# First attention: probabilities as TensorE's weights, values moving, no transposes of outputs, ten probability buffers

## The reference, cut to what matters

```python
qm, km, vm = (_split_heads(...) for ...)            # (4, 16, L, 8)
scores = jnp.einsum('bnlh,bnph->bnlp', qm, km) / np.sqrt(HEAD_DIM)
scores = jnp.where(mask, scores, MASK_FILL)
attn = jax.nn.softmax(scores, axis=-1)
out = jnp.einsum('bnlp,bnph->bnlh', attn, vm)
...
return out @ Wo.T + bo
```

## Time and profile before

| | before |
|---|---|
| median of 3 runs | 597.49 us (597.3 to 597.72) |
| profiled execution, its own time | 596.67 us |
| its span, first to last instruction | 594.9 us |
| mean granted clock of TensorE | 0.997 |
| TensorE busy | 569.7 us (96%) |
| VectorE busy | 401.7 us (68%) |
| ScalarE busy | 322.5 us (54%) |
| GpSimd busy | 105.4 us (18%) |

### The profile page before, as it was taken

One profiled execution on the slowest core, in us unless ns is written; L12 is line 12 of the kernel. 1 busy time (PEld: TensorE's weight loads), 2 busy tenths in 40 slices (PEclk: granted clock), 3 DMA queues, 4 the chain that ended last, 5 costly groups with the idle time before them and its releaser, 6 DMA issues.

```text
span 594.9 us, 8098 instructions
## 1 busy us (share of the span) xinstructions
PE 569.7 (96%) x2512; PEld 374.7 (63%) x2512; DVE 401.7 (68%) x1265; ACT 322.5 (54%) x566; POOL 105.4 (18%) x120
## 2 busy tenths in 40 slices
PE   4899999999999999999999899999899999999997
PEld 3556666665566667656676466666666676666664
DVE  6888989774132344666637585777889999768564
ACT  1587688766454476644855348745292542342321
POOL 3111110000111311242202432126201110100000
PEclk9999999999999999999999999999899999999999
DMA  4400000300311100101111011061321233341431
GB/s 119 195 15 10 18 10 2 105 39 19 107 36 35 54 20 19 36 28 54 60 31 44 14 42 44 1 199 39 122 75 51 90 119 98 111 138 62 143 120 56
DMA packets 23306, 38.35 MB, mean 64 GB/s; under 512 B 3776, under 2 KB 9536, under 8 KB 22880
## 3 DMA queue, kind: packets, MB, share of 16 engines
q1 hardware_dynamic: 22832, 37.44, 19.9%
q10 hardware_dynamic: 432, 0.40, 0.2%
HBM read 36.45 MB, written 1.38 MB: 64 GB/s over the span
## 4 chain that ended last, share of the span: by engine, by line
PE 80%; DVE 10%; ACT 4%; issue 2%; POOL 2%; DMA 1%; DVEq 0%; POOLq 0%; ACTq 0%
PE ps L1681 16%; PE ps L1493 9%; PE ps L1495 9%; PE ps L1851 9%; PE ps L1494 9%; PE ps L1488 3%; PE ps L1568 3%; PE ps L1588 3%; PE ps L1500 3%; PE ps L1603 2%; PE ps L1600 2%; PE ps L1758 1%; PE ps L1738 1%; DVE NM L1156 1%; PE ps L1530 1%
## 5 line engine op out<-in xcount | busy, mean ns | idle before, releaser
L1493 PE MATMUL ps<-xThi,w1s 128*128 128x512 f32 x256 | 147.5, 576 | 2.9 <-DVE h L1445 2.6
L911 ACT ACTIVATE h<-ps,early 128x512 f32<-128x512 f32 x128 | 86.7, 687 | 88.8 <-PE ps L1495 68.9
L1681 PE MATMUL ps<-h,w2s 128*128 128x512 f32 x256 | 122.5, 594 | 3.3 <-DVE ty L1245 3.2
L1495 PE MATMUL ps<-xTlo,w1s 128*128 128x512 f32 x256 | 101.4, 396 | 0.0
L1494 PE MATMUL ps<-xThi,w1s 128*128 128x512 f32 x256 | 100.9, 394 | 0.0
L1002 ACT ACTIVATE s<-ps 128x512 f32<-128x512 f32 x68 | 40.7, 598 | 95.4 <-PE ps L1495 93.8
L1493 PEld LDWEIGHTS ps<-xThi,w1s 128*128 128x128 f32 x256 | 48.5, 190 | 37.3 <-issue 18.2
L1681 PEld LDWEIGHTS ps<-h,w2s 128*128 128x128 f32 x256 | 46.2, 189 | 35.5 <-issue 23.8
L1494 PEld LDWEIGHTS ps<-xThi,w1s 128*128 128x128 f32 x256 | 48.7, 190 | 28.6 <-issue 24.3
L776 POOL TENSOR_TENSOR acc_o<-acc_o,ty 128x512 f32<-128x512 f32 x32 | 41.9, 1310 | 140.2 <-DVE ty L1245 115.7
L1445 DVE TENSOR_TENSOR h<-s,ps 128x512 f32<-128x512 f32 x68 | 46.5, 684 | 28.2 <-PE ps L1495 21.0
(11 more groups left out here) (264 smaller groups left out, 889.6 us busy)
## 6 DMA issues: line engine op xcount, KB each, us to landing
CB<-ct_rows SPq DMA_DIRECT2D x128, 128.0 KB, 2.9
WB<-wt_rows SPq DMA_DIRECT2D x32, 256.0 KB, 3.2
w2s<-w_dram SPq DMA_DIRECT2D x2, 2048.0 KB, 8.5
raw<-gu_dram SPq DMA_DIRECT2D x4, 512.0 KB, 3.8
x_in<-x_dram SPq DMA_DIRECT2D x4, 256.0 KB, 2.9
w2s<-dn_dram SPq DMA_DIRECT2D x1, 1024.0 KB, 5.7
out_dram<-ty SPq DMA_DIRECT2D x4, 256.0 KB, 2.9
late<-late_dram SPq DMA_DIRECT2D x1, 608.5 KB, 7.5
```

The source lines that it names most:

```text
L911: nc.scalar.activation(h32[:, c % HR, :], bank[c % 2], ACT.Gelu, bias=b1T[:, c:c + 1]).then_inc(b_gelu.sem, 1)
L1493: M(dst, w[0], xThi[:, x, :], start=start, stop=False)
L1495: return M(dst, w[0], xTlo[:, x, :], start=False, stop=stop)
L1681: M(bank[2], w2s[:, c * P:(c + 1) * P], h32[:, c % HR, :], start=(c % 4 == 0), stop=(c % 4 == 3)).then_inc(b_y.sem, 1)
```

## The change

VM keeps 16 columns for each head (8 values, 8 ones; VB goes from 32 to 16), VT becomes 128 x 64. In `values` the probabilities of a token tile (128 x 128 of a buffer of P32) are the weights and VT or VM moves: for each of four token tiles one product with VT (64 columns) and four with VM (16 columns each), added in bank 4, which then holds tokens by columns at once. The copy to OZ, its transposes, their signals and the tile OZ are gone; VectorE's `normalise` reads bank 4 directly. P32 gets the four buffers of CB too, ten in all. The value products of a group begin when all five exponentials are done. One memset of GpSimd goes, and the plans of all queues are written anew (not shown but for one line).

```diff
--- before.py
+++ after.py
@@ -103,231 +103,234 @@
 
 
 
+VB = 2 * HD
+
+
...
 PLAN_PE = {
...
+    "values": [[2730, 2800, 2869, 3163], [3475, 3550, 3605, 3715], [4103, 4233, 4351, 4429], [4646, 4701, 4756, 4905],
...
@@ -493,16 +496,15 @@
     KS = sb_a("KS", [P, NG, HG, KW], F32R)
     KST = sb_a("KST", [P, NG, HG * TP], F32R)
     VM = sb_a("VM", [P, NG, HG, VB])
-    VT = sb_a("VT", [P, NG, P])
+    VT = sb_a("VT", [P, NG, HG * VB])
     QN = [sb_a(f"QN{i}", [P, NT, NH, TP], F32R) for i in range(2)]
     QS = sb_a("QS", [P, NG, S], F32R)
     NM = sb_a("NM", [P, NT, NH])
-    OZ = sb_a("OZ", [P, S])
     w_out = sb_a("w_out", [P, P])
     rz = sb_a("rz", [P, NT, HG])
     ON = sb_a("ON", [P, NT, NG, HG * HD])
     q32, OT = xn, acc_o
-    P32 = [h32[:, i, :] for i in range(HR)] + [ty[:, i, :] for i in range(2)]
+    P32 = [h32[:, i, :] for i in range(HR)] + [ty[:, i, :] for i in range(2)] + [CB[:, i, :] for i in range(CR)]
     PR = len(P32)
     own_a.close()
 
@@ -569,7 +571,7 @@
     a_q2_ps, a_q2s = sig("a_q2_ps", NG), sig("a_q2s", NG)
     NU = HG + 1
     a_s_ps, a_exp = (sig(n, NG * NU) for n in ("a_s_ps", "a_exp"))
-    a_pv, a_oz, a_ozt_ps, a_on = sig("a_pv", NG), sig("a_oz", NG), sig("a_ozt_ps", NG), sig("a_on", 2 * NG)
+    a_pv, a_on = sig("a_pv", NG), sig("a_on", 2 * NG)
     a_ot_ps, a_ot = sig("a_ot_ps", 1), sig("a_ot", 1)
     a_y_ps, a_x1 = sig("a_y_ps", 1), sig("a_x1", 1)
 
@@ -617,7 +619,7 @@
 
     pieces1 = [(a["sh"][:, 0:2 * P], 2 * P, shs, 0)]
     pieces1 += [(a["gu"][:, 1024 * k:1024 * k + 1024], 1024, gus, 1024 * k) for k in range(NPIECE)]
-    NZERO, NONE, NPAD, NLATE = 7, 2 + 1 + HG + 1, 3, 2
+    NZERO, NONE, NPAD, NLATE = 6, 2 + 1 + HG + 1, 3, 2
 
     first_columns = width(EARLY[:[n for n, _, _ in EARLY].index("wo")])
 
@@ -736,8 +738,6 @@
             nc.gpsimd.memset(KS[:].bitcast(F32), 0.0).then_inc(zeros.sem, 1)
             yield
             nc.gpsimd.memset(VT[:], 0.0).then_inc(zeros.sem, 1)
-            yield
-            nc.gpsimd.memset(VM[:, :, :, 2 * HD:VB], 0.0).then_inc(zeros.sem, 1)
             yield
             nc.gpsimd.memset(QN[1][:, :, :, 28:TP].bitcast(F32), 0.0).then_inc(zeros.sem, 1)
 
@@ -863,9 +863,6 @@
                     act.wait_ge(a_pv.sem, (turn - PR) // NU + 1)
                 nc.scalar.activation(P32[turn % PR], bank[2 + n % 2], ACT.Exp,
                                      scale=float(1 / np.sqrt(HD))).then_inc(a_exp.sem, 1)
-            yield
-            act.wait_ge(a_pv.sem, a_pv.at(b, g + 1))
-            copy(OZ[:], bank[4]).then_inc(a_oz.sem, 1)
 
         def output(b):
             yield
@@ -1165,17 +1162,16 @@
                             qn[:, :, HG * g:HG * g + HG, 24:25].bitcast(F32), ALU.subtract).then_inc(a_nmq.sem, 1)
 
         def normalise(b, g):
-            src = four(bank[4])
-            yield
-            dve.wait_ge(a_ozt_ps.sem, a_ozt_ps.at(b, g + 1))
-
-            V.reciprocal(rz[:], src[:, :, HD::VB]).then_inc(a_on.sem, 1)
+            src = bank[4][:, 0:NT * HG * VB].rearrange("p (i h d) -> p i h d", i=NT, d=VB)
+            yield
+            dve.wait_ge(a_pv.sem, a_pv.at(b, g + 1))
+            V.reciprocal(rz[:], src[:, :, :, HD]).then_inc(a_on.sem, 1)
             yield
             dve.wait_ge(a_on.sem, a_on.at(b, 2 * g + 1))
             if b:
                 dve.wait_ge(a_ot_ps.sem, a_ot_ps.at(b, 0))
             V.tensor_tensor(ON[:, :, g, :].rearrange("p i (h d) -> p i h d", d=HD),
-                            src.rearrange("p i (h d) -> p i h d", d=VB)[:, :, :, 0:HD],
+                            src[:, :, :, 0:HD],
                             rz[:].unsqueeze(3).to_broadcast([P, NT, HG, HD]), ALU.mult).then_inc(a_on.sem, 1)
 
         def output(b):
@@ -1595,16 +1591,18 @@
                 pe.wait_ge(a_vtail.sem, a_vtail.at(b, HG))
             turn = (b * NG + g) * NU
             claim(4)
-            pe.wait_ge(a_exp.sem, turn + HG)
-            for j in range(HG):
-                M(bank[4][VB * j:VB * j + VB, :], VM[:, g, j, :], P32[(turn + j) % PR], start=True, stop=False)
-            yield
-            pe.wait_ge(a_exp.sem, turn + NU)
-            M(bank[4], VT[:, g, :], P32[(turn + HG) % PR], start=False, stop=True).then_inc(a_pv.sem, 1)
-            read_by(4, a_oz, a_oz.at(b, g + 1))
-            yield
-            claim(4)
-            transpose4(bank[4], OZ[:].rearrange("p (i t) -> p i t", i=NT)).then_inc(a_ozt_ps.sem, 1)
+            for i in range(NT):
+                if i:
+                    yield
+                else:
+                    pe.wait_ge(a_exp.sem, turn + NU)
+                t, o = slice(i * P, (i + 1) * P), i * HG * VB
+
+                M(bank[4][:, o:o + HG * VB], P32[(turn + HG) % PR][:, t], VT[:, g, :], start=True, stop=False)
+                for j in range(HG):
+                    last = M(bank[4][:, o + j * VB:o + (j + 1) * VB], P32[(turn + j) % PR][:, t], VM[:, g, j, :],
+                             start=False, stop=(j == HG - 1))
+            last.then_inc(a_pv.sem, 1)
             read_by(4, a_on, a_on.at(b, 2 * (g + 1)))
 
         def output(b):
```

More of the change, by code:

```diff
@@ L117 @@
-    "spread_second": [[37816, 38084, 38096, 38541, 38553, 40408, 40666, 41025, 41256, 41444, 41808, 42078, 42388,
[4 rows of a table removed]
+    "constants": [[6, 1272, 10517]],
+    "load_x": [[0], [1040], [2900], [4919]],
+    "load_context": [[1260], [4649], [7424]],
+    "second_weights": [[13555, 18775, 32218, 36037, 36431, 39895]],
+    "load_context1": [[14219], [15525], [32212], [33240]],
+    "store": [[45073], [50094], [55618], [56824]],
+    "spread_first": [[12886, 13561, 13567, 14213, 14787, 15453, 16288, 16910, 18194], [17939, 18188, 18769, 19433,
+        20613, 21284, 22425, 23072, 23924], [25345, 25587, 25593, 26031, 27237, 28134, 29289, 30216, 30955], [31958,
+        32200, 32206, 33234, 34497, 35030, 36437, 37119, 37784]],
@@ L122 @@
+    "spread_second": [[37790, 38191, 38203, 38215, 38227, 39748, 39883, 40073, 40477, 40731, 40869, 41352, 41607,
[4 rows of a table added]
 }
 PLAN_POOL = {
[L124 to L136, removed]
+    "constants": [[0, 15, 32, 60, 838, 866]],
+    "norm_a": [[710, 737], [1993, 2020], [3881, 3960], [7125, 7152]],
@@ new lines @@
+    "values": [[1712], [4980], [7822], [10564]],
+    "key_tails": [[1653, 1935], [3901, 6373], [6445, 7590], [10604, 10665]],
+    "norm_b": [[6242, 6269], [12549, 12576], [18895, 19343], [22551, 23198]],
+    "stage_b": [[14213, 14787, 15453, 16288, 16910, 17394, 18188, 18769], [20443, 20613, 21284, 22425, 23072, 24417,
+        24566, 25222], [26814, 27237, 28134, 29683, 30216, 30955, 31437, 32116], [34186, 34497, 35030, 36424, 37697,
+        38346, 38550, 39213]],
+    "split1": [[24345, 36181, 36679, 37973, 41262]],
@@ L137 @@
+    "stage_c": [[19215, 19242, 23299, 23327, 24217, 24244, 24973, 26376, 26403], [25650, 25678, 29442, 29478, 30611,
+        30638, 32245, 33083, 33110], [32586, 32614, 36053, 36080, 37566, 37593, 38217, 39339, 39366], [39685, 39713,
+        43474, 43501, 45378, 45405, 46378, 47662, 47689]],
+    "norm_d": [[29460, 29579], [36550, 36578], [41244, 41502], [48808, 48835]],
 }
@@ L168 @@
[L168 to L173, removed]
@@ new lines @@
+    "group": [[2322, 2429, 2478, 2537, 2592, 2652], [2991, 3131, 3180, 3279, 3328, 3399], [3497, 3735, 3827, 3879,
[5 rows of a table added]
+    "output": [[5107], [7975], [10833], [13302]],
+    "prepare_b": [[10986, 12129, 12823], [14414, 15022, 17875], [21730, 24181, 25282], [28474, 29313, 31895]],
+    "base": [[13483], [20380], [26750], [34123]],
+    "gelus": [[13082, 13352, 13552, 13621, 13776, 13844, 14055, 14210, 14662, 14784, 14852, 14965, 15168, 15450, 15594,
[9 rows of a table added]
+    "stage_c": [[14463, 14629, 16963, 17151, 19466, 19680, 19855, 19941], [26388, 26411, 26431, 26452, 26661, 27510],
+        [33238, 33261, 33281, 33302, 33511, 34662], [39406, 39428, 39590, 40313, 40540, 42161]],
@@ new lines @@
+    "exps_c": [[20157, 20330, 20794, 20982], [26862, 27032, 27562, 27803], [33813, 33983, 34476, 34734], [41035, 41205,
+        41620, 41808]],
+    "moves_c": [[20703, 21297, 21456, 21678], [27779, 28117, 28259, 28422], [34711, 35049, 35221, 35405], [41583,
+        41910, 42121, 42301]],
+    "cross": [[22053, 22528, 22697, 22736, 22775, 23269, 25391], [29033, 29456, 29495, 29534, 29573, 29908, 31843],
+        [35814, 36272, 36441, 36480, 36519, 36897, 38169], [43156, 43626, 43794, 43833, 43872, 44490, 46482]],
@@ L185 @@
[L185 to L190, removed]
-        ],
@@ L249 @@
-    "stage_d": [[40021, 40214, 40336, 40522, 40594, 40769, 40953, 41019, 41184, 41250, 41372, 41441, 41736, 41807,
[8 rows of a table removed]
+    "constants": [[0, 1037, 1047, 1248, 1256, 1264, 1305, 1343, 14203, 14946]],
+    "normalised": [[581, 672, 844, 863, 882, 906, 925, 976], [1654, 1748, 2215, 2268, 2351, 2376, 2460, 2556], [3624,
+        3842, 4067, 4104, 4149, 4417, 4462, 4856], [6997, 7087, 7312, 7681, 7699, 7724, 7743, 7794]],
```

(83 more changed lines are left out.)

98 lines of the change are left out of this document (17 added, 81 removed), and 180 rows, old and new, of tables (PLAN_ACT, PLAN_DVE, PLAN_PE, PLAN_SP).

## The result

The changed kernel takes 672.91 us (median of four, 662.81 to 676.68) against 597.39 us (the three executions from before and a fourth). Ratios and their intervals, here 1.116 (1.111 to 1.122), are taken over the executions within 1.5% of the fastest of each kernel, while medians are of all; this leaves out two of these four, and of the kernel before the one of 37 that took 647.2 us at a mean clock of 0.849. The forecast was 615.0 us, range 604 to 627. The direction was right, the time was 58 us too short. The profiled execution shows a span of 669.1 us and a mean granted clock of 0.911.

The account below looks back on a forecast made before the run. TensorE bounds the first attention at 83%, VectorE close behind at 80%. Span 594.9 + 28.8 of added TensorE work - 11.3 of gaps filled = 612.4 us, with 2.6 over the span 615.0 us; range 604 to 627.

Parts of the forecast that it names:

- What bounds the kernel: First attention: TensorE bounds it at 83%, VectorE close behind at 80%; after the change TensorE alone sets the pace.
- The 22 us of gaps: TensorE in the first attention: counted work fills 109 of 131 us, the other 22 us are gaps.
- The record price: New value products on TensorE: about 0.101 us a record, 4.1 us a group, 28.8 us added over 16 groups.
- Rival 1: Value products: weight loads hide and narrow products are cheap, so not slower, 592 or 575 us; chance 0.08.
- break-even of 0.0575 us: Record price of the new value products below which the change is not slower, from 2.30 us over 40 records.
- The gaps: First attention on TensorE: half of the gaps get filled, giving back 11.3 us.
- rival 4: Value products: few moving columns make the clock fall; all at half speed cost 66 us more, 680 us; chance 0.03.
- Ten buffers: Probability buffers, ten for six: exponentials never waited for value products, so the extra buffers can only fill gaps.
- rival 3: First attention: hardly any gaps fill and the mispriced order adds waits, 626 to 634 us; chance 0.08.
- Later stages: After the first attention: reordering put at 0, with bounds of plus or minus 3 us.

Follow-up runs that it names:

- the run without two heads: The 64-column form with the main value products of two heads of each group left out, against the kernel before: 598.4 us, ratio 1.001.
- the 64-column form: Changed kernel with every value product moving 64 columns, main ones zero outside the head's own 16; 626.9 us, 1.050 to the kernel before.
- The runs with more columns: Changed kernel with main value products widened by zeros from 16 to 32, 64 or 128 moving columns: 644.9, 626.9 and 628.7 us.
- the filler: Changed kernel plus one unneeded 256-column product of zeros ahead of each part of five value products; 661.6 us, 1.089 to the kernel before.

## Why the prediction was wrong, step by step

- **What bounds the kernel.** That with more work on TensorE no other engine matters was right; the run without two heads shows it for the 64-column form. The 22 us of gaps are the working's own figure, and no run shows them. They may be too large, since the sum has its pieces at their lowest prices: in the same chain two maxima right behind the value products took 0.49 us (at 82.88 us), not 0.30.
- **The record price.** Right: 0.101 forecast, 0.102 measured at the full clock, 4.08 us a group for 4.1. The estimate of 107 ns for a load by the Trainium skill (TensorE: Matmul & The Clock Gate, LDWEIGHTS) is near it. The 25 ns of its table of narrow products (Back-to-back issue gap) would have been too short by a factor of four; that section says that its table is of products without their loads. Rival 1 is out: the record price is far above its break-even of 0.0575 us.
- **The gaps.** Forecast 11.3 of 22 us filled. In the 64-column run, at 1.06 to 1.09 us a part, 31.0 to 33.0 us were added, and the attention's end moved by 28.7 us, at most 3.4 of them for the clock: 2 to 8 us filled. In the changed kernel 28.5 us were added and the end moved by 73.1; with all 56.3 us given to the clock 11.7 would be filled, with the 49 us estimated above 4. The term was too large by some 3 to 9 us, which the range would have covered.
- **The clock: the step that failed.** The sum has no term for it: a fall of the clock was put at nothing and left to rival 4, "Narrow products keep few columns moving", with a chance of 0.03. Measured were up to 112.6 us at 1.2 GHz and some 49 us, at most 56, of added time. The mechanism was on paper, and the chance was far too low. That its price, 66 us and a time of 680, comes near is luck: it has the value products alone at half speed and all the time, where the trace shows every product of the stretch at half speed for part of the time. The reason given was that "the narrow products of the trace left the clock at full". Those were single pieces of 0.8 us among full-width products. They could price a record, and could not say what 64 parts of such records do to the clock in a stretch where they take half of TensorE's time. The runs with more columns show the cause in the new order, with loads and records unchanged; the filler shows, in two executions of four, that narrow products can pass at the full clock when other work stands between them.
- **Ten buffers.** Right that they give nothing in the old order (597.3 us). Not foreseen: with the swapped products, order and buffers together save 28 to 40 us, part of it clock.
- **The mispriced order** (rival 3) was no cause of note: TensorE was idle for 3.2 of the 205 us from 16 to 221. Later stages, forecast at 0 within 3 us: plus 1.1 us.

What would beat both kernels was not found. By these prices no swap with 40 loads a group can: 40 loads of 128 columns cost 4.1 us a group at the full clock, where 2.30 us stood.

## What to carry to other kernels

Before making the large operand the weights, count weight loads: here each record with a load of 128 columns cost 0.10 to 0.11 us, whether 16 or 128 columns moved. Then ask how such records would lie: single narrow pieces in a trace price a record, and do not show that the clock stays up when they take half of the time. Give its fall a term or a real chance; it takes every other product in the stretch with it. A busy row of nines does not exclude it: read the granted clock beside it.

## What the runs showed of the hardware

- TensorE, without idle time by its records, was granted 1.2 GHz for 37 us on end (90 to 127 us) in a stretch where 72 of its 156 records had 16 moving columns. The first such fall after the value products had begun came at 45 to 50 us, behind 5 us in which TensorE had been busy for all of 5. The Trainium skill (TensorE: Matmul & The Clock Gate, What's actually happening) says that the gate goes by how busy the engine has been recently; by the busy time of the profile, weight loads included, this trace does not agree.

```profile
90.00:127.00 37.00, 37.00 (x156) 34.65 (x156) 15.76 (x55) 11.68 (x22) 1.97 (x4) 0.50 0.01 4
```

- Columns of zeros made a difference to the clock: with 64 moving columns, 48 of them zeros, it was 1.00 from 50 to 125 us, where 16 without those zeros gave 0.65; the filler is nothing but zeros. Whether other values would do as much was not run.
- More moving columns cost little time: eight records took 0.85 us with 16 columns and 0.89 with 64, beside weight loads of 128 columns. With 128 columns they took 0.89 too (the chain of that run at 60.76 us).
